# Self-attention of a decoder layer: the first copy of a tile's turned probabilities moved ahead in ScalarE's order

## The chip, the cores and the metric

The kernel runs on one core of a Trainium2 chip. The time is that of one execution on the device in microseconds (us), the median of several runs. Beside it there is one profiled execution with a trace of every instruction. The engines are PE (TensorE, matmuls), DVE (VectorE), ACT (ScalarE), POOL (GpSimd) and SP (SyncE, which only issues DMAs here). Each runs its own list of instructions in order; they wait for one another by semaphores.

## The reference

One decoder layer on 2048 tokens of width 256 (32 sequences of 64), in three parts, each with a layer norm ahead and a residual behind:

```python
x = x + attn(layernorm(x))      # 16 heads of 16, quantised activations and weights
x = x + xattn(layernorm(x), ctx)  # 16 heads of 128, 64 context rows a sequence
x = x + ffn(layernorm(x))       # 8 experts of 688, the best 2 of each token
```

The change is in the first. Its projections are "bitlinear": the input is normalised, multiplied by a gain, scaled by 127 over its largest magnitude in the row, rounded to integers, and multiplied by weights that are rounded to -1, 0 and 1. Scores are taken within a sequence, softmax, values, and the output goes through a fourth bitlinear.

```python
scores = einsum('bhtd,bhsd->bhts', Q, K) / sqrt(16)
out = einsum('bhts,bhsd->bhtd', softmax(scores), V)
return bitlinear(out, wo, go)
```

## The kernel before, in words

The program has three stages in a row: the self-attention (function `attention`, to about 209 us of the trace), the cross-attention and the experts. All engines meet between stages. The self-attention also prepares operands of the later stages: ten pieces of weights and context are split into a high and a low half (`split_high` on ACT, `split_low` on POOL), and the products of value and output weights are formed and split (`value_weights`, `value_high`, `value_low`).

The tokens are 16 tiles of 128 rows (two sequences each). `attention` writes one loop over steps t = -4 to 15 for each engine, and the order of the calls in that loop is the order of the engine's work. It is a software pipeline: in step t the engines begin tile t + 4 and finish tile t. Things that are done for two tiles at once (`pair(t, lag)`) come every second step. For ACT a step is (before the change):

- `squares` (even steps): sums of squares of the attention's output, two tiles, and two small exponents of them (L327 to L331)
- `turned_probs(t, 0)`: copy of the first half of the turned probabilities out of the bank `pt` (L321), 128x512
- `value_high` (odd steps, L357), `quantise(t + 4)` (L297, three instructions, which wait for the scales of DVE's `front`), `turned_probs(t, 1)`: the copy of the second half
- `query(t + 2)` (L307), `exponent(t + 1)` (L316), `value(t + 2)` (L312), `key_scales(t + 3)` (L302)
- `quantise_out` (odd steps, L336), `split_high` (odd steps, L352 and L353, 128x1024 each)
- `second_norm` (even steps from 6 on, L340 and L341) and `h_high` (L346)

PE in a step: `turn_probs(t, 0)` (L545, 16 small matmuls, 32 rows of the trace, that turn half of the heads' probabilities into the bank `pt`), `value_weights` and `project_out` (odd steps), `scores(t + 1)` (L560), `turn_probs(t, 1)`, which must wait until ACT has copied the first half out of the same bank, `project(t + 2)` (L572), `values(t + 2)` (L580), `key_scales(t + 3)` (L586), and `outputs(t)` (L596, probabilities times values), which needs both halves copied. `turn_probs(t + 1, 0)` comes behind `outputs(t)` and needs the exponents of tile t + 1.

DVE in a step: `front(t + 4)` (L426 to L432, the input with gain, and its scales), `residual` and `value_low` (odd), `shifted(t + 1)` (L449, L452), `keys(t + 2)` (L444), `out_scale` (odd, L466 to L472), `second_stats` (even), `integers(t + 4)` (L438), `outputs(t)` (L457, L461), `out_integers` (odd, L477, which waits for `quantise_out`), `hidden` (even from 6 on, L500, which waits for `second_norm`). All of it is in that order whatever comes ready first.

The copy and its waits are these:

```python
def turned_probs(i, part):
    act.wait_ge(p_done, 2 * i + part + 1)
    need(act, o_done, i)
    nc.scalar.copy(pT[:, 8 * part:8 * part + 8, :]...,
                   pt[:, :]).then_inc(pT_done, 1)
```

`p_done` counts PE's turned halves, `o_done` its `outputs`.

Of the kernel before, what the change touches and what calls it, by code (L numbers as in the profile page):

```python
# [92 lines left out]
def need(engine, semaphore, count):  # L93

    if count > 0:
        engine.wait_ge(semaphore, count)


def attention(nc, sem, dram, x_sb, cst, ao, hT, wq, wk, wvo, cT, ck, carry):
# [5 lines left out]
    with ctx:  # L105
# [67 lines left out]
        def tile(i):  # L173
            return 0 <= i < NT

        def pair(t, lag):

            j, rest = divmod(t - lag, 2)
            return j if rest == 0 and 0 <= j < NPAIRS else None
# [8 lines left out]
        with nc.Block() as block:  # L188
# [81 lines left out]
            def _(act):  # L270
# [23 lines left out]
                def quantise(i):  # L294
                    act.wait_ge(sc_done, 2 * i + 2)
                    for j in range(QKV):
                        nc.scalar.activation(u[:, j, :], u[:, j, :], ACT.Identity, scale=qsc[:, i, j:j + 1], bias=magic).then_inc(yq_done, 1)  # L297

                def key_scales(i):
                    act.wait_ge(t_done, i + 1)  # L300
                    need(act, kf_done, i - 1)
                    nc.scalar.copy(dk[i % 2][:, :], g0[:, 0:P]).then_inc(zT_done, 1)  # L302

                def query(i):
                    act.wait_ge(q_done, i + 1)
                    need(act, s_done, i - 1)
                    nc.scalar.copy(q_f[i % 2][:, :, :].rearrange("p m n -> p (m n)"), qb[:, :]).then_inc(qf_done, 1)  # L307

                def value(i):
                    act.wait_ge(v_done, i + 1)  # L310
                    need(act, o_done, i - 2)
                    nc.scalar.activation(vb[i % 3][:, :, 0:D1], g2[:, 0:C].rearrange("p (h d) -> p h d", d=D1), ACT.Identity, scale=deq[:, i, 2:3]).then_inc(vb_done, 1)  # L312

                def exponent(i):
                    act.wait_ge(sub_done, i + 1)
                    nc.scalar.activation(sp[i % 2][:, :, :], sp[i % 2][:, :, :], ACT.Exp, scale=deq[:, i, 0:1]).then_inc(exp_done, 1)  # L316
# [4 lines that stand above are left out]
                    nc.scalar.copy(pT[:, 8 * part:8 * part + 8, :].rearrange("p h n -> p (h n)"), pt[:, :]).then_inc(pT_done, 1)  # L321

                def squares(j):
                    act.wait_ge(ao_done, 2 * j + 2)
                    for a in range(2):
                        need(act, sq_done, 2 * j + a)
                        nc.scalar.activation(junk[:, :], ao2[j % 2][:, a, :], ACT.Square, accum_out=ssq[:, j, a:a + 1]).then_inc(sq_done, 1)  # L327
                    act.wait_ge(sq_done, 2 * j + 2)
                    links.link(nc.scalar.activation(ln_o[:, j, :], ssq[:, j, :], ACT.Ln, scale=1.0 / C, bias=cst[:, CONSTS + 1:CONSTS + 2]))
                    nc.scalar.activation(rms_o[:, j, :], ln_o[:, j, :], ACT.Exp, scale=0.5).then_inc(rms_done, 1)  # L330
                    nc.scalar.activation(rrms_o[:, j, :], ln_o[:, j, :], ACT.Exp, scale=-0.5).then_inc(rms_done, 1)  # L331

                def quantise_out(j):
                    act.wait_ge(so_done, 2 * j + 2)
                    for a in range(2):
                        nc.scalar.activation(ug[:, a, :], ug[:, a, :], ACT.Identity, scale=qsc_o[:, j, a:a + 1], bias=magic).then_inc(yo_done, 1)  # L336

                def second_norm(j):
                    act.wait_ge(st_done, 2 * j + 2)
                    links.link(nc.scalar.activation(ln_h[:, j, :], mv_o[:, j, :, 1], ACT.Ln, bias=cst[:, CONSTS:CONSTS + 1]))  # L340
                    nc.scalar.activation(rstd_h[:, j, :], ln_h[:, j, :], ACT.Exp, scale=-0.5, bias=cst[:, CONSTS + 6:CONSTS + 7]).then_inc(rs_done, 1)  # L341

                def h_high(j):
                    act.wait_ge(h_done, 2 * j + 2)
                    need(act, hT_in, 32 * j)
                    nc.scalar.copy(hp[:, :, 0, :], h[:, :, :]).then_inc(hh_done, 1)  # L346

                def split_high(n):
                    act.wait_ge(raw_in[n % 2], (n // 2 + 1) * 16)
                    src, high, low, up, parts = splits[n]  # L350
                    part = raw[n % 2][:, :].rearrange("p (a n) -> p a n", a=parts) if parts > 1 else raw[n % 2][:, :]
                    nc.scalar.mul(high, part, up).then_inc(high_done, 1)  # L352
                    nc.scalar.mul(part, part, up).then_inc(up_done, 1)  # L353

                def value_high(n):
                    act.wait_ge(vo_done, n + 1)
                    nc.scalar.mul(wvo[:, 0, 2 * n:2 * n + 2, :], g1[:, :].rearrange("p (h o) -> p h o", h=2), W_UP).then_inc(vo_high, 1)  # L357

                for t in steps:
                    if pair(t, 2) is not None:  # L360
                        squares(pair(t, 2))
                    if tile(t):
                        turned_probs(t, 0)
                    if pair(t, 1) is not None:
                        value_high(pair(t, 1))
                    if tile(t + 4):
                        quantise(t + 4)
                    if tile(t):
                        turned_probs(t, 1)
                    if tile(t + 2):  # L370
                        query(t + 2)
                    if tile(t + 1):
                        exponent(t + 1)
                    if tile(t + 2):
                        value(t + 2)
                    if tile(t + 3):
                        key_scales(t + 3)
                    if pair(t, 3) is not None:
                        quantise_out(pair(t, 3))
                    if t % 2 and 0 <= (t + 3) // 2 < NSPLIT:  # L380
                        split_high((t + 3) // 2)
                    if pair(t, 6) is not None:
                        second_norm(pair(t, 6))
                        h_high(pair(t, 6))
# [1573 lines left out]
```

## Time and profile before

| | |
|---|---|
| three runs | 847.98, 848.79, 852.25 us, median 848.79 |
| the profiled execution | 852.5 us, its span in the trace 850.4 us |
| busy in the span | PE 722.7, DVE 568.7, ACT 453.9, POOL 382.5 us |
| mean granted TensorE clock | 0.935 of 2.4 GHz |
| the self-attention | from the start to about 209 us |

Times of the trace count from the span's start. In a row of a timeline the first number is when the instruction (or a group of the same line, "x32") started, the second how long it took, and in brackets stands how long the engine had been idle before it and what ended that.

### The profile page before, as it was taken

Reading aid. Unit: us, or ns where it says so; the run is one execution under the profiler, and the core shown is the slowest. Engines: PE = TensorE matmul, PEld = TensorE weight load, DVE = VectorE, ACT = ScalarE, POOL = GpSimd, SP = SyncE. Lnnn points to the kernel's source line nnn. Section 1 sums busy time; section 2 is a strip of 40 time slices with the busy share of each in tenths; the row PEclk is TensorE's granted clock in tenths of the full one; section 3 lists DMA queues with packets and bytes.
Section 4 is the critical chain, followed back from the end, with each engine's and each line's share of the span. In section 5 each row is a group of like instructions: output and inputs, shape, how many; then the busy total and the mean of one; then the engine's idle time right before and its main releaser. Section 6 shows DMA issues by size and latency. Waiting matters only on the chain. (4 is left out here: it accounts for less than half of the span.)

```text
span 850.4 us, 26921 instructions
## 1 busy us (share of the span) xinstructions
PE 722.7 (85%) x10796; PEld 522.1 (61%) x10796; DVE 568.7 (67%) x1052; ACT 453.9 (53%) x875; POOL 382.5 (45%) x462
## 2 busy tenths in 40 slices
PE   0499888887887999999999996988199999998993
PEld 0388777775443566656556664766167777776772
DVE  5778788863886989999898997967853333332330
ACT  0567777764785666667675763544023333333331
POOL 0112222322585555555555555620056666665753
PEclk9879999995998999999999998999599999999997
DMA  9312222321664757576757573619949988889882
GB/s 323 112 50 56 59 52 64 66 58 20 168 194 156 186 127 180 135 187 160 191 128 173 163 167 112 223 31 406 369 89 158 149 147 143 142 128 137 145 140 40
DMA packets 192471, 121.91 MB, mean 143 GB/s; under 512 B 140800, under 2 KB 172800, under 8 KB 192224
## 3 DMA queue, kind: packets, MB, share of 16 engines
q1 hardware_dynamic: 178928, 103.54, 50.3%
q0 software_dynamic: 7488, 9.32, 7.1%
q10 hardware_dynamic: 5936, 7.34, 2.5%
q8 instruction: 90, 1.47, 0.7%
q14 instruction: 29, 0.24, 0.1%
HBM read 61.04 MB, written 27.00 MB: 104 GB/s over the span
## 5 line engine op out<-in xcount | busy, mean ns | idle before, releaser
L1754 DVE SCALAR_TENSOR_TENSOR f_slot_work<-psu,f_slot_work 128x688 f32<-128x688 f32 x39 | 34.1, 875 | 109.8 <-PE psu L1825 109.8
L1350 PE MATMUL xbank_a<-arena,x_o 128*128 128x256 f16 x768 | 96.6, 277 | 5.7 <-DVE x_o L1155 2.9
L1572 POOL DMA_INDIRECT out_dram<-f_y,f_to x39 | 62.2, 1595 | 71.8 <-DMA out_dram<-f_y,f_to 55.4
L1350 PEld LDWEIGHTS xbank_a<-arena,x_o 128*128 128x128 f16 x768 | 73.4, 99 | 28.7 <-DVE x_o L1155 10.3
L1254 PE MATMUL xbank_qk<-arena 128*128 128x512 f16 x336 | 84.8, 390 | 4.6 <-PEq L188 4.3
L1841 PE MATMUL fbank<-arena,f_slot_work 128*128 x663 | 79.2, 274 | 3.3 <-DMA f_slot_work<-hid_hl 3.3
L1825 PE MATMUL psg<-wgu,f_slot_work 128*128 x468 | 74.7, 309 | 2.5 <-DMA f_slot_work<-rows_in 2.0
L1825 PE MATMUL psu<-wgu,f_slot_work 128*128 x468 | 74.6, 309 | 0.0
L1841 PEld LDWEIGHTS fbank<-arena,f_slot_work 128*128 128x128 f16 x663 | 64.7, 98 | 14.6 <-issue 4.3
L1622 ACT CAST hid_hl<-f_slot_work 128x688 f16<-128x688 f32 x39 | 29.8, 765 | 77.4 <-DVE f_slot_work L1754 75.4
L915 POOL TENSOR_TENSOR arena<-arena,cst 128x512 f32<-128x512 f32 x25 | 26.0, 1039 | 92.2 <-DVE cT L1190 92.2
L961 ACT ACTIVATE sqq<-xbank_qk 128x512 f32<-128x512 f32 x56 | 33.3, 595 | 56.3 <-PE xbank_qk L1254 56.3
L1615 ACT ACTIVATE f_slot_work<-psg 128x688 f32<-128x688 f32 x39 | 29.0, 743 | 64.4 <-PE psg L1825 63.1
L545 PE MATMUL bank_pt<-cst,sp 64*64 64x64 f32 x1024 | 42.8, 242 | 21.6 <-ACT pT L321 19.4
L1825 PEld LDWEIGHTS psg<-wgu,f_slot_work 128*128 128x128 f16 x468 | 45.4, 98 | 23.4 <-issue 3.8
L1825 PEld LDWEIGHTS psu<-wgu,f_slot_work 128*128 128x128 f16 x468 | 45.8, 98 | 22.5
L1757 DVE TENSOR_TENSOR hid_hl<-f_slot_work,hid_hl 128x688 f16<-128x688 f32 x39 | 34.2, 877 | 32.4 <-ACT hid_hl L1622 32.4
L545 PEld LDWEIGHTS bank_pt<-cst,sp 64*64 64x64 f32 x1024 | 38.4, 154 | 23.9 <-issue 20.5
L1254 PEld LDWEIGHTS xbank_qk<-arena 128*128 128x128 f16 x336 | 28.7, 99 | 36.8 <-issue 8.0
L1145 DVE TENSOR_TENSOR q_hl<-xbank_qk,q_hl 128x512 f16<-128x512 f32 x56 | 38.4, 686 | 16.9 <-ACT q_hl L962 16.9
L1262 PE MATMUL xbank_qk<-cT,wk 128*128 128x512 f16 x168 | 47.1, 391 | 0.0
L904 POOL TENSOR_TENSOR x_pf<-x_sc,x_rden 128x512 f32<-128x512 f32 x32 | 33.4, 1042 | 29.8 <-DVE x_rden L1178 29.8
(285 smaller groups left out, 1717.5 us busy)
## 6 DMA issues: line engine op xcount, KB each, us to landing
arena<-in_wx SPq DMA_DIRECT2D x51, 256.0 KB, 3.0
wgu<-w_hl SPq DMA_DIRECT2D x2, 5504.0 KB, 26.5
ao<-key_norms SPq DMA_DIRECT2D x64, 128.0 KB, 3.3
w_hl<-cT SPq DMA_DIRECT2D x26, 256.0 KB, 2.1
w_hl<-x_pair SPq DMA_DIRECT2D x25, 256.0 KB, 2.2
ao<-in_wx SPq DMA_DIRECT2D x10, 256.0 KB, 3.2
w_hl<-ao SPq DMA_DIRECT2D x10, 256.0 KB, 2.1
x_sb<-in_x SPq DMA_DIRECT2D x4, 512.0 KB, 9.6
```

The lines of the kernel that those rows point to most:

```text
L545: last = nc.tensor.matmul(pt[rows, n * S:(n + 1) * S], sp[i % 2][rows, 8 * part + n, :], cst[rows, IDENT + S * b:IDENT + S * b + S], start ...
L904: nc.gpsimd.tensor_tensor(pf[:, :, :], sc[n % 2][:, :, :], rden[n % 2][:, :].unsqueeze(2).to_broadcast([P, 2 * GT, S]), ALU.mult).then_inc ...
L961: nc.scalar.activation(sqq[h % 2][:, :], query_bank(h), ACT.Square, scale=1.0 / (H_UP * W_UP)).then_inc(sq_done, 1)
L1145: nc.vector.tensor_tensor(q_hl[:, 1, slot(h), :], query_bank(h), q_hl[:, 0, slot(h), :], ALU.subtract).then_inc(lq_done, 1)
L1254: last = nc.tensor.matmul(query_bank(h), wq[:, a, k, f:f + D2], hT[:, g, b * NCH + k, :], start=(j == 0), stop=(j == len(terms) - 1))
L1262: last = nc.tensor.matmul(key_bank(h), wk[:, a, f:f + D2], cT[:, g, b, :], start=(j == 0), stop=(j == 2))
L1350: last = nc.tensor.matmul(acc[t // 2][:, (t % 2) * C:(t % 2 + 1) * C], o_hl[h % 2][:, a, at:at + P], wvo[:, b, e, :], start=(e == 0 and j ...
L1572: nc.gpsimd.indirect_dma_start(out=dram["out_rows"], out_offset=bass.IndirectOffsetOnAxis(ap=to[n % 2][:, 0:1], axis=0), in_=y[n % 2][:, : ...
L1754: nc.vector.scalar_tensor_tensor(out=h3, in0=psu[:, :].rearrange("p (c n) -> p c n", c=2)[:, :, 0:FH], scalar=HID_UP / (H_UP * W_UP), in1= ...
L1757: nc.vector.tensor_tensor(hid_hl[n % 2][:, 1, 0:FF], hid[n % 2][:, :], hid_hl[n % 2][:, 0, 0:FF], ALU.subtract).then_inc(s["hh_low"], 1)
L1825: last = nc.tensor.matmul(bank[:, c * 512:c * 512 + FH], xT[n % 2][:, b * NCH + k, :], wgu[:, bass.ds(e, 1), at:at + FH].rearrange("p a n ...
L1841: last = nc.tensor.matmul(ps[n % 2][:, 0:C], hidT[n % 3][:, a, f, :], wd[:, bass.ds(e, 1), at:at + C].rearrange("p a n -> p (a n)"), start ...
```

## The change

Both calls at the head of ACT's step are moved. The copy of the first half is now made for tile t + 1 at the end of step t, behind `key_scales`, and so a step earlier in the list: ahead of `quantise_out`, `split_high`, `second_norm` and `h_high` of step t. The squares stay in their step, but go from its head to behind that copy.

```diff
                 for t in steps:
-                    if pair(t, 2) is not None:
-                        squares(pair(t, 2))
-                    if tile(t):
-                        turned_probs(t, 0)
                     if pair(t, 1) is not None:
                         value_high(pair(t, 1))
...
                     if tile(t + 3):
                         key_scales(t + 3)
+                    if tile(t + 1):
+                        turned_probs(t + 1, 0)
+                    if pair(t, 2) is not None:
+                        squares(pair(t, 2))
                     if pair(t, 3) is not None:
                         quantise_out(pair(t, 3))
```

In the lists that follow `u` is the tile being quantised, `pT` and `bank_pt` the turned probabilities and their bank, `a_raw` a piece to split, `ao` and `k_hl` space that holds the attention's output, the quantised output and the hidden rows, `per_pair` small numbers of a pair. First ACT from the end of step 9 into step 10, before:

```order
L302 COPY dk<-bank_g 128x128
L336 ACTIVATE k_hl<-k_hl,cst,per_pair 128x256 x2
L352 ACTIVATE cT<-a_raw 128x2x512
L353 ACTIVATE a_raw<-a_raw 128x1024
L327 ACTIVATE k_hl,per_pair<-ao_0 128x256 x2
L329 ACTIVATE per_pair<-per_pair,cst 128x2
L330 ACTIVATE per_pair<-per_pair 128x2
L331 ACTIVATE per_pair<-per_pair 128x2
L321 COPY pT<-bank_pt 128x512
L297 ACTIVATE u<-u,cst,qsc 128x256 x3
L321 COPY pT<-bank_pt 128x512
```

The same place in the changed kernel:

```order
L302 COPY dk<-bank_g 128x128
L321 COPY pT<-bank_pt 128x512
L336 ACTIVATE k_hl<-k_hl,cst,per_pair 128x256 x2
L352 ACTIVATE cT<-a_raw 128x2x512
L353 ACTIVATE a_raw<-a_raw 128x1024
L297 ACTIVATE u<-u,cst,qsc 128x256 x3
L321 COPY pT<-bank_pt 128x512
```

The copy of tile 10's first half (the first L321) has passed quantising and weight piece, and the squares (L327 to L331) have left this place.

ACT at the end of step 10, before:

```order
L302 COPY dk<-bank_g 128x128
L340 ACTIVATE per_pair<-k_hl,cst 128x2
L341 ACTIVATE per_pair<-per_pair,cst 128x2
L346 CAST k_hl<-k_hl 128x2x256
L321 COPY pT<-bank_pt 128x512
L357 ACTIVATE arena<-bank_g 128x512
```

and in the changed kernel:

```order
L302 COPY dk<-bank_g 128x128
L321 COPY pT<-bank_pt 128x512
L327 ACTIVATE k_hl,per_pair<-ao_0 128x256 x2
L329 ACTIVATE per_pair<-per_pair,cst 128x2
L330 ACTIVATE per_pair<-per_pair 128x2
L331 ACTIVATE per_pair<-per_pair 128x2
L340 ACTIVATE per_pair<-k_hl,cst 128x2
L341 ACTIVATE per_pair<-per_pair,cst 128x2
L346 CAST k_hl<-k_hl 128x2x256
L357 ACTIVATE arena<-bank_g 128x512
```

Here tile 11's copy and the squares of step 10 stand ahead of the second norm (L340, L341), which stood directly behind L302. The lists of PE, DVE, POOL and SP are the same in both kernels.

## Rows read from the trace of the kernel before

**Rows 1.** Waits of PE inside the self-attention (us in total, times, longest).

```profile
PE bank_pt L545 <- ACT pT L321: 19.4, 7, 3.2
```

**Rows 2.** Timeline of PE, steps 10 to 12 (start, us, engine, line).

```profile
143.76 1.15 PE L545 MATMUL bank_pt<-cst,sp 64*64 64x64 f32 x32 [0.30 <-ACT sp L316]
...
149.74 1.97 PE L545 MATMUL bank_pt<-cst,sp 64*64 64x64 f32 x32 [3.19 <-ACT pT L321]
...
153.75 2.04 PE L596 MATMUL bank_g<-vb,pT 64*64 64x17 f32 x64
155.63 1.13 PE L545 MATMUL bank_pt<-cst,sp 64*64 64x64 f32 x32
...
158.19 1.72 PE L560 MATMUL bank_s<-k_f,q_f 32*64 32x64 f32 x64
159.84 1.15 PE L545 MATMUL bank_pt<-cst,sp 64*64 64x64 f32 x32
...
162.36 2.04 PE L596 MATMUL bank_g<-vb,pT 64*64 64x17 f32 x64
164.70 1.15 PE L545 MATMUL bank_pt<-cst,sp 64*64 64x64 f32 x32 [0.30 <-ACT sp L316]
```

**Rows 3.** Timeline of ACT, steps 9 to 10.

```profile
144.54 1.09 ACT L336 ACTIVATE k_hl<-k_hl,cst,per_pair 128x256 f32<-128x256 f32 x2 [0.32 <-DVE per_pair L472]
...
147.44 0.40 ACT L327 ACTIVATE k_hl<-ao 128x256 f32<-128x256 f32 x1
...
149.03 0.57 ACT L321 COPY pT<-bank_pt 128x512 f32<-128x512 f32 x1
149.50 1.58 ACT L297 ACTIVATE u<-u,cst,qsc 128x256 f32<-128x256 f32 x3
...
155.08 0.30 ACT L340 ACTIVATE per_pair<-k_hl,cst 128x2 f32<-128x2 f32 x1 [0.20 <-DVE k_hl L492]
155.41 0.30 ACT L341 ACTIVATE per_pair<-per_pair,cst 128x2 f32<-128x2 f32 x1
```

**Rows 4.** Timeline of DVE, steps 9 and 10.

```profile
145.67 0.43 DVE L477 TENSOR_SCALAR k_hl<-k_hl 128x512 bf16<-128x512 f32 x1
...
148.41 0.19 DVE L432 SCALAR_TENSOR_TENSOR deq<-amax,norm,wm 128x3 f32<-128x3 f32 x1
...
156.47 0.73 DVE L500 TENSOR_SCALAR k_hl<-x_sb,k_hl,per_pair 128x256 f32<-128x256 f32 x2
```

**Rows 5.** Timelines of PE and DVE, the first pairs.

```profile
63.82 1.13 PE L545 MATMUL bank_pt<-cst,sp 64*64 64x64 f32 x32
...
71.84 2.04 PE L596 MATMUL bank_g<-vb,pT 64*64 64x17 f32 x64
...
91.26 2.19 PE L596 MATMUL bank_g<-vb,pT 64*64 64x17 f32 x64
...
101.91 1.13 PE L545 MATMUL bank_pt<-cst,sp 64*64 64x64 f32 x32
...
83.28 0.43 DVE L477 TENSOR_SCALAR k_hl<-k_hl 128x512 bf16<-128x512 f32 x1
...
103.64 0.43 DVE L477 TENSOR_SCALAR k_hl<-k_hl 128x512 bf16<-128x512 f32 x1
...
114.49 0.73 DVE L500 TENSOR_SCALAR k_hl<-x_sb,k_hl,per_pair 128x256 f32<-128x256 f32 x2
```

**Rows 6.** Timelines of DVE, PE and POOL, the last pairs and the stage's end.

```profile
177.19 0.73 DVE L500 TENSOR_SCALAR k_hl<-x_sb,k_hl,per_pair 128x256 f32<-128x256 f32 x2
...
192.88 3.60 PE L596 MATMUL bank_g<-vb,pT 64*64 64x17 f32 x64 [0.67 <-ACT pT L321]
...
207.05 2.12 POOL L257 TENSOR_TENSOR ck<-a_raw,ck 128x1024 f16<-128x1024 f32 x1 [7.28 <-ACT a_raw L353]
```

**Rows 7.** A row of PE's timeline; busy by stretch (PE, PEld, DVE, ACT, POOL, granted clock, DMA).

```profile
67.86 1.97 PE L545 MATMUL bank_pt<-cst,sp 64*64 64x64 f32 x32 [1.26 <-ACT pT L321]
...
149.74:153.20 3.46, 3.46 (x48) 3.34 (x49) 1.22 (x1) 2.41 (x5) 2.37 (x2) 0.52 0.19 43
```

## The prediction, made before the changed kernel ran

> **What bounds the kernel now.** I first asked whom TensorE waits for inside the self-attention. The table of waits [rows 1] names the first copy of turned probabilities, line 321: 19.4 us in 7 waits. That is all the change can take away directly. Then I read one pair of tiles, t = 10 and 11, on the timelines of three engines. I write tp0(t), tp1(t) for TensorE's two turns of a tile's probabilities (L545), TP0, TP1 for ScalarE's copies of them (L321), outputs(t) for L596, hidden(t) for VectorE's L500 in step t.
>
> On PE [rows 2] tp0(10) starts at 143.76, and tp1(10) only at 149.74, after 3.19 us idle and at half clock (1.97 us, where 159.84 shows 1.15). Outputs(10) starts at 153.75, tp0(11) at 155.63. From tp1(11) at 159.84 to outputs(11) at 162.36 PE needs 2.52 us when nothing stops it. On ACT [rows 3] the copy for which PE waits starts at 149.03, because output quantising and a weight piece (144.54 to 147.44, 2.90 us) and the squares (147.44 to 149.03, 1.59 us) lie ahead of it. The second norm is at 155.08, 0.63 us to the end of its last row. On DVE [rows 4] L477 (the integers of the output) starts at 145.67, 1.13 us after ACT's quantising, the scales of tile 14 are done at 148.60, and hidden(10) starts at 156.47. The pair comes round in some 21.0 us: tp0(12) is at 164.70 [rows 2].
>
> **The change, part by part.** No instruction is added or removed. On ACT 16 copies of 0.58 us stand elsewhere, and 7 groups of squares. PE, DVE, POOL and SP issue the same rows in the same order, so no DMA is passed by another. Two waits of others change hands.
>
> *TP0 goes ahead of quantising and weight piece (all pairs).* Gain: PE no longer waits for it; the stall of 3.19 us goes. Price: ACT now waits for PE at that place, and what is queued behind the copy comes later. Behind it is the quantising of the output (L336), for which DVE waits at L477, and behind L477 stands L426 to L432, the scales of the next tile. Worked for t = 10: tp0 ends near 144.9, the copy takes ACT until 145.43 (0.05 to start, 0.48 to the next, as 149.03 to 149.50), quantising starts 0.89 later than before, so L477 at 146.56 and the scales at 149.49. ACT is free at 145.43 + 2.90 = 148.33 and must wait for them: the quantising of tile 14 (L297) starts at 149.50, exactly as before. Its 1.50 us and the copy TP1 (0.58) give outputs(10) at 151.65, 2.1 us earlier than 153.75.
>
> *Squares go behind the next TP0, and so does the second norm.* This is the new wait. Outputs(10) at 151.65, tp0(11) 1.88 later at 153.53, its end and the copy 1.15 + 0.05 + 0.48 later: 155.2. Then squares 1.59, second norm 0.63, and 0.08 to DVE: hidden(10) starts at 157.5, against 156.47 before. DVE, which has its own outputs(10) done some 0.7 us after PE's (151.65 + 2.04 + 0.7 = 154.4), stands still for 3 us, and behind hidden is the next tile's L426. So the 3.19 us stall is paid back with 1.0 us on top: a pair that has a second norm takes 22.0 us. In the present trace that norm hid in ACT's wait for tp0(11); that cover is gone.
>
> *The sum by pairs, with TensorE at full clock.* The second norm is only there for t = 6, 8, 10, 12, 14.
> - t = 2: from tp0(2) at 63.82 [rows 5], 1.13 + 0.05 + 0.48, weight piece 1.9 (2.90 less the 1.0 of L336), tile quantising 1.50, copy 0.63: outputs(2) at 69.5 instead of 71.84. PE then has no gap, so tp0(4) is 2.2 earlier, at 79.7.
> - t = 4: L477 at 79.7 + 1.66 + 1.1 = 82.45 (83.28 before), scales 2.93 later, outputs(4) at 87.5 instead of 91.26; tp0(6) 3.85 earlier, at 98.05 (101.91 before).
> - t = 6: the same way L477 100.8 (103.64), outputs(6) 105.9, hidden(6) 5.86 later (1.88 + 1.68 + 1.59 + 0.63 + 0.08) at 111.8 instead of 114.49: 2.7 ahead.
> - t = 8 and 10: 1.0 lost each. Ahead 0.7.
> - t = 12 has no tile to quantise: TP1(12) is at 169.3, PE is ready at about 170.4 itself, hidden(12) at 176.3 instead of 177.19 [rows 6]: 0.9 gained. Ahead 1.6.
> - t = 14: hidden(12) to tp0(14) is the 8.23 us from hidden(10) to tp0(12) less 2.5 for the missing scales plus 0.4 for ACT's copies: 6.15. Then 1.68, 2.90 and 0.63: outputs(14) 11.4 after hidden(12), against 15.7 (192.88 - 177.19). It takes 2.04 instead of 3.60 if the clock is up: 5.85 gained.
> - Tail: the stage ends with POOL's last low piece, which starts 10.6 us after outputs(14) ended (207.05 against 192.88 + 3.60). Squares, second norm, hidden and two copies now follow tp0(15) in a row: about 0.5 more.
> Sum: 2.7 - 2.0 + 0.9 + 5.85 - 0.5 = 6.95 us faster. What follows the stage starts after its last engine and moves as a block; I cost it at nothing.
>
> *The clock.* A stall that goes should also take away the slow stretch behind it, but the walk leaves new gaps on PE. From the start of tp0(10) PE needs 1.08, the scores' 1.65 (158.19 to 159.84) and 2.52, together 5.25 us, to be ready for outputs(10), that is at 149.0, and gets its copy at 151.6: a gap of 2.6 us, and it lies straight ahead of outputs(10) and tp0(11), which are on the path. A second one of about 2 us is before outputs(11). [Rows 7]: behind 1.26 us idle tp1(2) ran at 1.97 us a group, so a gap shorter than these sufficed for the fall to 1.2 GHz; 0.30 us before tp0(10) did not. A fall lasts about 3.4 us (granted 0.52 from 149.74 to 153.20), which costs at most 3.46 x 0.48 = 1.7 us. Bounds for the even gap: 0 (it falls into work with slack) and 1.7; I take 1.3, since 3.2 us of path work stand right behind it. For the odd gap 0 and 1.2; I take 0.5, since outputs(11) has 0.9 us of slack before tp0(12). Count: t = 4 at 1.7 (PE is the bound right after), t = 6, 8, 10 at 1.3, odd gaps at t = 7, 9, 11 at 0.5, and 2.35 at t = 14 and the tail (outputs(14) at 3.60 as now, and 0.8 on tp0(15)): 9.45 us. It is as large as everything else together.
>
> The Trainium skill ("TensorE: Matmul & The Clock Gate", section "Why this matters for your kernels") ties the fall to idle gaps longer than any that I work out here. By that rule the 9.45 us would be nothing and the change would come out 7 us faster. The 1.26 us row speaks against it, so it is only a rival.
>
> **Sum:** 6.95 - 9.45 = -2.5, that is 2.5 us slower. The profiled execution took 852.5 us (span 850.4 and 2.1 around it), 3.7 above the median of 848.79; a difference worked out in the one I add to the other: 851.3 us.
>
> **The rivals.**
> *The clock stays up:* no cost behind the gaps, 848.8 - 6.95 = 841.8 us. For it: the new gaps are shorter than 3.19 us and lie spread. Against it: the 1.26 us row. 0.14.
> *Slower, the clock falls behind both gaps of every pair at its full price:* 4 x 1.7, 3 x 1.2, 2.35 and 1.0 at t = 12 make 13.75, and the time 855.6 us. For it: the even gap is followed by nothing but path work. Against it: slow stretches eat the next gap. It decides from a clock cost of 11.2 us on (6.95 + 4.25), that is when the even gap costs 1.7 and the odd one about 1. 0.26.
> *Nothing takes the place of the stall:* the whole 19.4 us go, 829.4 us. Against it: DVE's order puts hidden ahead of the next tile, and ACT's order the norm behind the squares. 0.04.
>
> **How the numbers follow.** The forecast, a change of little size, has 0.56; its own range is 848 to 854.5. Half a per cent, 4.2 us, is about what a measurement of this kernel can tell from no change, so "same" is 844.6 to 853.0. Faster: 0.14 + 0.04 = 0.18. Slower: 0.26 and 0.07 of the forecast's upper end, 0.33. Same: 0.49. The range reaches to most of both clock rivals: 843.5 to 856.5; what is left out is the fastest part of the first, the top of the second and the last.
>
> **What would show it.** Right: the waits of tp1 for L321 are gone; DVE waits 3 us before hidden (L500) on L341 in five steps; ACT waits for tp0 before every first copy; L477 waits for L336; outputs(even) waits for TP1; pairs t = 8 and 10 come round in 22.0 us at full clock and 23 to 24 with slow stretches, and those before t = 6 in less than now. Wrong: if hidden doesn't wait for the norm; if outputs(even) starts without a gap; if the pairs from t = 8 on take 21 us or less; if the stages behind the self-attention change their length by over a microsecond.

## The result, and the profile after

| | before | changed |
|---|---|---|
| median | 852.20 us (20 runs) | 856.29 us (20 runs) |
| ratio | | 1.0053, 95% interval 1.0031 to 1.0075 |
| profiled execution, span | 850.4 us | 850.3 us |
| mean granted TensorE clock | 0.935 | 0.923 |
| TensorE busy | 722.7 us | 731.3 us |

The changed kernel is slower by half a per cent: 4.5 us on the 848.79 that the prediction started from (2.6 to 6.4), so 853.3 us. One of the 20 executions of the kernel before took 1354 us, and the ratio leaves it out. The 853.3 us lie in the range, just above what I called "same" (844.6 to 853.0), and the likeliest case, no change that a measurement can tell, was not what came: the interval leaves no change out. The sum itself said 2.5 us slower, so its direction was right and its size was not.

One trace of each doesn't show the difference in the span, because the first two tiles happened to take 3.9 us less in the changed kernel's trace (tp0(2) starts at 59.92 against 63.82 [rows 5]), where the order is all but the same; in a second trace of the changed kernel (e8 below) tp0(2) starts at 63.86. Counted from tp0(2) to the end of POOL's last low piece the self-attention took 145.35 us before and 151.80 after.

The waits inside the self-attention, in the changed kernel (us in total, times, longest):

```profile
PE bank_g L596 <- ACT pT L321: 8.3, 8, 2.6
...
DVE k_hl L500 <- ACT per_pair L341: 16.4, 5, 3.8
...
DVE k_hl L477 <- ACT k_hl L336: 8.8, 6, 1.8
...
ACT pT L321 <- PE bank_pt L545: 29.6, 18, 4.3
```

The 19.4 us in which PE waited for the first copy [rows 1] are gone. In their place PE waits 8.3 us for the second copies ahead of outputs, DVE waits 16.4 us at hidden for the second norm, which it never did, and 8.8 us at L477 for the output quantising. ACT itself waits 29.6 us for PE's turned halves.

PE's timeline in the same pair, t = 10 and 11, and the next (start, us, engine, line, idle before):

```profile
143.73 1.97 PE L545 MATMUL bank_pt<-cst,sp 64*64 64x64 f32 x32 [0.57 <-ACT sp L316]
...
148.36 1.97 PE L545 MATMUL bank_pt<-cst,sp 64*64 64x64 f32 x32
...
152.85 2.04 PE L596 MATMUL bank_g<-vb,pT 64*64 64x17 f32 x64
154.74 1.13 PE L545 MATMUL bank_pt<-cst,sp 64*64 64x64 f32 x32
...
162.82 0.38 PE L580 MATMUL bank_g<-k_hl,zT 128*128 128x256 bf16 x2 [1.73 <-DVE x_sb L483]
...
164.03 2.04 PE L596 MATMUL bank_g<-vb,pT 64*64 64x17 f32 x64 [0.55 <-ACT pT L321]
166.90 1.97 PE L545 MATMUL bank_pt<-cst,sp 64*64 64x64 f32 x32 [0.83 <-ACT sp L316]
...
176.10 2.25 PE L596 MATMUL bank_g<-vb,pT 64*64 64x17 f32 x64
178.20 1.12 PE L545 MATMUL bank_pt<-cst,sp 64*64 64x64 f32 x32
```

ACT's in the same pair:

```profile
145.75 0.59 ACT L321 COPY pT<-bank_pt 128x512 f32<-128x512 f32 x1 [1.55 <-PE bank_pt L545]
146.23 1.09 ACT L336 ACTIVATE k_hl<-k_hl,cst,per_pair 128x256 f32<-128x256 f32 x2
...
150.32 1.58 ACT L297 ACTIVATE u<-u,cst,qsc 128x256 f32<-128x256 f32 x3 [1.10 <-DVE deq L432]
151.81 0.56 ACT L321 COPY pT<-bank_pt 128x512 f32<-128x512 f32 x1
...
155.91 0.59 ACT L321 COPY pT<-bank_pt 128x512 f32<-128x512 f32 x1 [1.49 <-PE bank_pt L545]
...
158.32 0.30 ACT L341 ACTIVATE per_pair<-per_pair,cst 128x2 f32<-128x2 f32 x1
```

DVE's, with hidden(8), hidden(10) and hidden(12):

```profile
135.49 0.74 DVE L500 TENSOR_SCALAR k_hl<-x_sb,k_hl,per_pair 128x256 f32<-128x256 f32 x2 [2.81 <-ACT per_pair L341]
...
147.36 0.43 DVE L477 TENSOR_SCALAR k_hl<-k_hl 128x512 bf16<-128x512 f32 x1 [1.78 <-ACT k_hl L336]
...
158.65 0.73 DVE L500 TENSOR_SCALAR k_hl<-x_sb,k_hl,per_pair 128x256 f32<-128x256 f32 x2 [2.99 <-ACT per_pair L341]
...
182.11 0.73 DVE L500 TENSOR_SCALAR k_hl<-x_sb,k_hl,per_pair 128x256 f32<-128x256 f32 x2 [2.99 <-ACT per_pair L341]
```

Compare with [rows 2 to 4]. tp0(10) starts at 143.73, by chance almost where it did before (143.76), so the numbers can be read side by side. TP0(10) is now at 145.75, L336 at 146.23 instead of 144.54, and L477 follows it at 147.36 instead of 145.67. The quantising of the next tile starts at 150.32 (149.50), TP1(10) at 151.81 and outputs(10) at 152.85, still 0.9 earlier than 153.75. But TP0(11), squares and second norm now stand in a row, 155.91 to 158.62, and hidden(10) starts at 158.65 instead of 156.47.

The granted clock in two stretches of the changed kernel and, third, in one of the kernel before (us, PE, PEld, DVE, ACT, POOL busy, then clock and DMA):

```profile
142.48:152.72 10.24, 9.67 (x164) 9.14 (x160) 8.11 (x19) 7.53 (x13) 2.28 (x2) 0.50 0.35 59
166.34:176.59 10.25, 9.69 (x158) 9.06 (x158) 6.30 (x14) 7.17 (x13) 3.36 (x2) 0.50 0.39 68
...
190.66:200.88 10.22, 9.55 (x134) 8.33 (x129) 1.63 (x7) 3.79 (x7) 2.10 (x2) 0.50 0.07 15
```

Before, the slow stretch of a pair lasted 3.4 us (0.52 from 149.74 to 153.20, [rows 7]). Here two of them last 10.2 us each. The first begins at 142.5, inside outputs(9), behind gaps of 1.61 and 0.60 us; the second at 166.3, behind gaps of 1.73 and 0.55 us and inside a third of 0.83 us, in which PE waited for the exponents of tile 12. Each ends only about when outputs(even) begins: tp0, scores, tp1 and project all run at 1.2 GHz. Over the stage the falls last 6.8, 6.8, 6.8, 10.2, 10.2 and 13.7 us, and the last one 4.4 us up to the stage's end. A long stretch was there before the change, too: the third row, behind a gap of 2.86 us at tp1(14), is a part of the old trace from which the prediction took only outputs(14) at 3.60 us.

This is also why outputs(10) has no gap ahead of it: PE, at half clock from tp0(10) on, was itself ready no earlier than the copy, which ended at 152.37. The forecast gap of 2.6 us ahead of outputs(even) opened at t = 4 and 6 (2.55 us each) and not at t = 8, 10 and 12.

The stage piece by piece. "Walk" is the prediction's sum at full clock, "forecast" the same with its clock terms:

| stretch | before | walk | forecast | after |
|---|---|---|---|---|
| tp0(2) to tp0(4) | 18.09 | 15.9 | 15.9 | 15.74 |
| tp0(4) to tp0(6) | 20.00 | 18.35 | 20.05 | 21.49 |
| tp0(6) to hidden(6) | 12.58 | 13.75 | 15.05 | 16.03 |
| hidden(6) to hidden(8) | 21.03 | 22.0 | 23.8 | 22.31 |
| hidden(8) to hidden(10) | 20.95 | 22.0 | 23.8 | 23.16 |
| hidden(10) to hidden(12) | 20.72 | 19.8 | 20.3 | 23.46 |
| hidden(12) to the end of outputs(14) | 19.29 | 13.45 | 15.0 | 15.82 |
| from there to POOL's end | 12.69 | 13.2 | 14.0 | 13.79 |
| sum | 145.35 | 138.45 | 147.9 | 151.80 |

### The profile page after: what moved, and what is told of

Read it like the earlier page. It is cut to its first block and busy times, and to the rows that moved or that the text cites. A ratio compares the mean times of both kernels' runs of the same rounds, so it can differ in the third digit from the quotient of the medians.

```text
span 850.3 us, 26921 instructions
## 1 busy us (share of the span) xinstructions
PE 731.3 (86%) x10796; PEld 528.4 (62%) x10796; DVE 569.5 (67%) x1052; ACT 453.1 (53%) x875; POOL 379.2 (45%) x462
## 5 line engine op out<-in xcount | busy, mean ns | idle before, releaser
L545 PE MATMUL bank_pt<-cst,sp 64*64 64x64 f32 x1024 | 44.9, 250 | 5.0 <-ACT sp L316 5.0
L1155 DVE SCALAR_TENSOR_TENSOR x_o<-xbank_o,x_o 128x512 f16<-128x512 f32 x55 | 37.8, 687 | 11.1 <-ACT x_o L972 11.1
```

The costliest lines, as they stand in the source:

```text
L545: last = nc.tensor.matmul(pt[rows, n * S:(n + 1) * S], sp[i % 2][rows, 8 * part + n, :], cst[rows, IDENT + S * b:IDENT + S * b + S], start ...
L1155: nc.vector.scalar_tensor_tensor(out=o_hl[h % 2][:, 1, :].rearrange("p (b n) -> p b n", b=2), in0=ob_of(h)[:, :, 0:RW], scalar=1.0 / P_UP, ...
```

## The experiments

Two things moved together: the copy, and the squares, which took the second norm with them by standing ahead of it. And beside the waits there is the clock. The theory was: the new waits of DVE (for the norm at hidden, for the quantising at L477) take the place of the stall, and slow stretches behind the new gaps take the rest. The first rival was that the clock alone cost, the second that every delay of the norm costs what it saves.

All edits are to ACT's loop unless another place is named. Ratios are to the kernel before, run beside each on the same chip; the pairs are from hidden(6) to (8), (10), (12) and (14) in the trace, and the stage from tp0(2) to POOL's end, with the granted clock in it:

| kernel | median us | ratio (95%) | pairs, us | stage, us (clock) |
|---|---|---|---|---|
| before | | 1 | 21.03, 20.95, 20.72, 19.97 | 145.35 (0.88) |
| changed | 856.29 | 1.0053 (1.0031 to 1.0075) | 22.31, 23.16, 23.46, 20.40 | 151.80 (0.81) |
| e1 norm first | 841.58 | 0.9885 (0.9855 to 0.9915) | 20.04, 21.33, 17.04, 15.79 | 135.01 (0.88) |
| e2 copy alone | 859.37 | 1.0057 (1.0024 to 1.0090) | 21.49, 22.36, 19.23, 19.31 | 152.62 (0.83) |
| e3 squares alone | 840.52 | 0.9882 (0.9824 to 0.9940) | 19.91, 19.91, 19.91, 17.00 | 133.73 (0.87) |
| e5 norm, then squares | 836.02 | 0.9775 (0.9725 to 0.9825) | 19.46, 18.13, 19.46, 16.93 | 129.80 (0.92) |
| e6 copy behind quantising | 833.87 | 0.9817 (0.9763 to 0.9870) | 18.18, 18.50, 16.28, 14.83 | 120.29 (0.98) |
| e7 copy ahead of quantising | 844.28 | 0.9870 (0.9815 to 0.9924) | 20.01, 21.34, 17.03, 16.99 | 135.95 (0.88) |
| e4 all gaps filled | 854.49 | 1.0015 (0.9977 to 1.0053) | 23.13, 22.50, 21.88, 18.54 | 147.61 (0.95) |
| e10 even gap filled | 864.21 | 1.0105 (1.0043 to 1.0166) | 25.63, 25.07, 26.21, 22.40 | 158.04 (0.83) |
| e11 both gaps, fewer | 860.63 | 1.0079 (1.0043 to 1.0115) | 24.52, 24.96, 24.27, 21.17 | 154.39 (0.86) |
| e12 e5 and a filled gap | 833.45 | 0.9769 (0.9727 to 0.9811) | 18.19, 20.77, 17.77, 16.36 | 126.80 (0.95) |

**e1, the norm ahead of the copy.**

```diff
 # on the changed kernel
                         key_scales(t + 3)
+                    if pair(t, 6) is not None:
+                        second_norm(pair(t, 6))
                     if tile(t + 1):
                         turned_probs(t + 1, 0)
...
                     if pair(t, 6) is not None:
-                        second_norm(pair(t, 6))
                         h_high(pair(t, 6))
```

> The changed kernel with the second norm (L340, L341) ahead of the next tile's first copy instead of behind the squares; the cast of the hidden rows stays at the step's end. Theory (what takes the place of the removed stall is DVE's wait for the second norm, 16.4 us in 5 waits): these waits go, a pair with a norm comes round about 3 us sooner at full clock, and the whole is 10 to 15 us faster than the changed kernel, ratio to the kernel before 0.985 to 0.995. Rival (only TensorE's slow stretches behind the new gaps cost): the gap before outputs(even) stays 2.5 us, the stretches stay, and the time is within 3 us of the changed kernel's.

It came to 841.58 us, ratio 0.9885, some 1.7% under the changed kernel. A wait of DVE, two rows of DVE's timeline (L478 is L477 here, L501 is L500) and outputs(10) on PE:

```profile
DVE k_hl L478 <- ACT k_hl L336: 8.2, 6, 1.5
...
141.62 0.43 DVE L478 TENSOR_SCALAR k_hl<-k_hl 128x512 bf16<-128x512 f32 x1 [1.50 <-ACT k_hl L336]
...
150.97 0.73 DVE L501 TENSOR_SCALAR k_hl<-x_sb,k_hl,per_pair 128x256 f32<-128x256 f32 x2
...
146.69 3.60 PE L597 MATMUL bank_g<-vb,pT 64*64 64x17 f32 x64 [2.55 <-ACT pT L321]
```

The waits at hidden are gone (no idle time before 150.97), while L477's are nearly as they were (8.2 for 8.8 us). Outputs(10) now has a gap of 2.55 us ahead of it, as outputs(4) and outputs(6) have in the changed kernel too, and runs at half clock. About 14 us went (1.7% by the two ratios), so the time is the theory's and not the rival's. But the clock did not stay as it was. From tp0(2) to the stage's end, in the kernel before, the changed one, e1 and e4 (below):

```profile
63.82:209.17 145.35, 119.79 (x2920) 110.23 (x2916) 105.12 (x219) 99.68 (x207) 37.95 (x30) 0.88 0.25 54
...
59.92:211.72 151.80, 130.22 (x2920) 118.73 (x2917) 106.74 (x219) 98.71 (x207) 38.16 (x30) 0.81 0.23 52
...
60.23:195.24 135.01, 118.24 (x2920) 107.78 (x2916) 106.56 (x219) 98.39 (x207) 38.00 (x30) 0.88 0.29 58
...
62.96:210.57 147.61, 137.62 (x3148) 123.55 (x3145) 107.00 (x219) 98.39 (x207) 38.16 (x30) 0.95 0.25 53
```

Twice the length, times what the clock lacks to 1, is the time at 1.2 GHz: about 35, 58, 32 and 15 us. So e1 took away the norm's waits and some 25 us of slow clock together, and alone it can't part the two. e4 parts them roughly: it keeps the waits at hidden (15.2 us) and takes away more slow time than e1, and its stage is 4.2 us shorter than the changed kernel's, where e1's is 16.8 us shorter. The larger part of e1's gain is therefore that of the waits; how much exactly isn't shown, since e4 pays for its fillers.

**e2, the copy alone** (squares back at the head of ACT's step).

```diff
 # on the changed kernel
                 for t in steps:
+                    if pair(t, 2) is not None:
+                        squares(pair(t, 2))
                     if pair(t, 1) is not None:
...
                         turned_probs(t + 1, 0)
-                    if pair(t, 2) is not None:
-                        squares(pair(t, 2))
```

> The changed kernel with the squares back at the head of ACT's step; only the copy is moved. Theory: the norm then waits for the copy alone, hidden comes 1.6 us sooner and the tile's quantising starts up to 0.5 us later, so about 1.1 us a pair, 5 to 8 us faster than the changed kernel, ratio to before 0.995 to 1.000. Rival (the copy ahead of output quantising is what costs, by way of L477): no change against the changed kernel, ratio 1.005.

1.0057, the rival's number: no gain over the changed kernel. Waits of PE and DVE:

```profile
PE bank_g L596 <- ACT pT L321: 16.6, 7, 2.9
...
DVE k_hl L500 <- ACT per_pair L341: 10.2, 5, 2.2
DVE k_hl L477 <- ACT k_hl L336: 7.6, 6, 1.9
```

Hidden waits 2.2 us where it waited 2.8 to 3.8, so 0.6 to 1.6 us less a wait (10.2 in five), but PE's waits for the second copies doubled to 16.6 us. That this is because the squares stand ahead of the next tile's quantising is my reading of the order. The pairs from hidden(6) on are shorter, while what lies before is longer: hidden(6) starts 60.8 us after tp0(2), against 53.3 in the changed kernel, at a granted clock of 0.76 against 0.87, with one slow stretch of 17 us in it. So both places tried for the squares with the copy moved cost about as much: ahead of the norm and ahead of the quantising.

**e3, the squares alone** (the copy at its old place).

```diff
 # on the kernel before
                 for t in steps:
-                    if pair(t, 2) is not None:
-                        squares(pair(t, 2))
                     if tile(t):
                         turned_probs(t, 0)
...
                         key_scales(t + 3)
+                    if pair(t, 2) is not None:
+                        squares(pair(t, 2))
                     if pair(t, 3) is not None:
```

> The kernel before with only the squares moved behind the key scales; the copy stays at the head of the next step. Theory: PE's stall for the first copy shrinks from 3.2 to 1.6 us, DVE's hidden waits about 1 us for the norm, and a pair is some 1 us shorter: 4 to 7 us faster than before, ratio 0.992 to 0.996. Rival (every delay of the norm costs what it saves): ratio 0.999 to 1.003, with 1.6 us of waits before hidden.

0.9882, better than expected. The waits, and tp1(10) in the same pair:

```profile
PE bank_pt L545 <- ACT pT L321: 5.2, 5, 1.4
...
DVE k_hl L500 <- ACT per_pair L341: 2.2, 3, 1.2
...
140.09 1.97 PE L545 MATMUL bank_pt<-cst,sp 64*64 64x64 f32 x32 [0.51 <-ACT pT L321]
```

PE's stall for the first copy fell from 19.4 to 5.2 us, tp1 waits 0.51 us where it waited 3.19, and hidden waits for the norm only 2.2 us in three steps. Three of the four pairs take 19.91 us. The clock has hardly a part in it: 0.87 in the stage against 0.88 before, while the stage is 11.6 us shorter. So the half of the change that moved the squares gains 1.2% by itself, and moving the copy as well turns that into a loss of 0.5%.

**e5, the norm first, then the squares, the copy at its old place.**

```diff
 # on e3
                         key_scales(t + 3)
+                    if pair(t, 6) is not None:
+                        second_norm(pair(t, 6))
                     if pair(t, 2) is not None:
                         squares(pair(t, 2))
...
                     if pair(t, 6) is not None:
-                        second_norm(pair(t, 6))
                         h_high(pair(t, 6))
```

> The kernel before with the squares moved to the step's end, behind the second norm (which keeps its place) and ahead of the cast of the hidden rows; the copies stay. Theory: both waits go, PE's for squares (3.2 us down to at most 1.4) and DVE's for the norm (2.2 us in all in the run with the squares ahead of it): 0 to 3 us faster than that run, ratio to before 0.984 to 0.990. Rival (the norm's place is worth nothing once the copy stays): same as that run, 0.988, with DVE idle for PE instead.

836.02 us, 0.9775: both kernels are beaten, the changed one by 2.8%. The ratio is below the range that I gave. It puts e5 9 us below e3, where the stages in the two traces differ by 3.9 us, and the two intervals touch. DVE no longer waits for the norm. What is left of PE's wait (L546 is L545 here), and tp1(even) of one pair:

```profile
PE bank_pt L546 <- ACT pT L321: 8.5, 6, 1.6
...
138.51 1.15 PE L546 MATMUL bank_pt<-cst,sp 64*64 64x64 f32 x32 [1.58 <-ACT pT L321]
```

**e7, the copy ahead of the output quantising, and e6, behind it,** both on e5. Only the copies for even tiles move here, which pass the quantising and the weight piece; those for odd tiles stay at the head of the step. Nothing delays the norm.

```diff
 # on e5; e7 as here, e6 with the two calls in the other order
-                    if tile(t):
+                    if tile(t) and t % 2:
                         turned_probs(t, 0)
...
+                    if t % 2 and tile(t + 1):
+                        turned_probs(t + 1, 0)
                     if pair(t, 3) is not None:
                         quantise_out(pair(t, 3))
```

> As before that, but the copy ahead of output quantising, as in the changed kernel. It shows the price of the copy's move alone, without any delay of the norm. Theory: DVE waits 1 us or more at L477 in six steps, the next tile's scales come that much later: 4 to 9 us slower than with the copies at their old place, ratio 0.991 to 0.999. Rival (only the norm behind the squares cost in the change): within 2 us of the run with the copies at their old place.

> As the run with norm, then squares, and in odd steps the next tile's first copy between output quantising and weight piece. Theory: L477 is not delayed and PE's last waits for L321 go (5.2 us in five waits), but the next tile's quantising still waits for DVE's scales, so 0 to 3 us faster than that run, ratio 0.981 to 0.989. Rival: the gap only moves to outputs(even), as in the changed kernel, with slow stretches behind it: slower than that run by 1 to 4 us.

e7 took 844.28 us, 0.9870, against 0.9775 for e5. Its waits (L599 and L480 are L596 and L477 here):

```profile
PE bank_g L599 <- ACT pT L321: 12.5, 7, 2.5
...
DVE k_hl L480 <- ACT k_hl L336: 9.1, 6, 1.7
```

PE's 8.5 us at tp1 are gone, DVE has 9.1 us at L477 instead and PE 12.5 us at outputs, against 1.6 in e5. That is the copy's price without the norm, about 1% by the ratios, whose intervals just touch; the stage is 6.2 us longer, and its lower clock (0.88 against 0.92) is a part of that. With the quantising first (e6) L477 doesn't wait (0.5 us, as before the change), and the time, 833.87 us and 0.9817, can't be told from e5. The trace says more than that: e6's four pairs are 6.2 us shorter together than e5's, at a granted clock of 0.98 in the stage against 0.92, while its tp0(2) starts 6.2 us later (68.85 against 62.69), behind first tiles that ran at 1.2 GHz until 67.1. Whether such first tiles belong to e6's order or fell that way in this one execution wasn't tried, so whether passing the weight piece alone gains anything stays open.

**e4, e10, e11, the clock.** On the changed kernel, matmuls whose results nobody reads were put on PE, into free columns of a bank that PE owns at that moment.

```diff
 # in PE's part
+                def busy(bank, count):
+                    for _ in range(count):
+                        nc.tensor.matmul(bank[:, 272:512], w_int[:, 0, 0:P], w_int[:, 1, 0:240], start=True, stop=True)
...
                 def outputs(t, i):
+                    need(pe, ao_done, i)
+                    need(pe, vo_low, passed(t, 1))
+                    if i > 3:
+                        busy(g1, 20 if i % 2 == 0 else 12)   # e10: 20, 0; e11: 20, 5
```

In e4 six more stand before tp0(even). The two waits ahead of the fillers are ones that outputs has anyway, asked for earlier.

> The changed kernel with matmuls of no use (128x240, into free columns of a bank that PE owns at that time) in the gaps that it opened: 20 before outputs(even), 12 before outputs(odd), 6 before tp0(even), from tile 4 on. Theory (slow stretches behind the new gaps cost about 10 us of the stage): granted clock 1.00 there, the pairs t = 8 and 10 come round in 22.0 us, and the whole is 7 to 11 us faster than the changed kernel, ratio to before 0.993 to 0.998. Rival (the waits of DVE alone cost, the slow stretches hide in slack): within 2 us of the changed kernel, ratio 1.005.

> The changed kernel with 20 matmuls of no use (128x240) in the gap before outputs(even) alone, from tile 4 on, none elsewhere. Theory (slow stretches behind that gap cost about 1.5 us a pair or more, and the additions elsewhere in the earlier run with busy gaps cost 0.5 us a pair themselves): 5 to 9 us faster than the changed kernel, ratio to before 0.995 to 1.001. Rival: the slow stretches move behind the odd gap, 1.003 to 1.006.

> The changed kernel with 20 matmuls of no use before outputs(even) and 5 before outputs(odd), none before tp0, so that both new gaps are filled without delaying what follows. Theory (slow stretches behind the odd gap cost as much as those behind the even one): pairs t = 8 and 10 in 22.0 to 22.6 us, ratio to before 0.996 to 1.002, better than with the even gap alone (1.0105) by 5 us or more. Rival (useless matmuls only shift the slow stretches): pairs over 23 us, ratio above 1.003.

From hidden(8) to hidden(10), first the changed kernel (in each row the stretch and its length, then PE, PEld, DVE, ACT, POOL busy, clock, DMA):

```profile
135.49:158.65 23.16, 20.38 (x450) 18.73 (x442) 17.68 (x37) 15.46 (x33) 5.77 (x5) 0.78 0.31 56
```

With all gaps filled (e4):

```profile
138.44:160.94 22.50, 21.16 (x462) 18.45 (x456) 17.59 (x37) 15.45 (x33) 5.76 (x5) 0.93 0.23 52
```

The clock is up at 0.93 from 0.78, the pair takes 22.50 us, and the walk had said 22.0 at full clock; the rest I put down to the fillers (outputs(9) and tp0(10) each start some 0.7 us late behind them, partly hidden). From tp0(2) the stage took 147.6 us instead of 151.8, and the whole was measured at 1.0015 instead of 1.0053. That misses my forecast (0.993 to 0.998, clock 1.00), and by time alone e4 decides nothing: its interval holds the changed kernel's 1.0053 as well. It is the trace that says that the slow stretches cost about 4 us at the least. The waits of DVE are still there (15.2 us at hidden, 10.9 at L477). How much more the clock costs is hidden by the fillers that stand on PE's path.

The other two missed by more. e10, rows of PE around the odd gap, and the pair:

```profile
142.34 0.38 PE L587 MATMUL bank_g<-k_hl,zT 128*128 128x256 bf16 x2 [1.72 <-DVE x_sb L483]
...
143.85 3.32 PE L607 MATMUL bank_g<-vb,pT 64*64 64x17 f32 x64 [0.91 <-issue]
...
202.26 3.86 PE L541 MATMUL bank_g<-k_hl 128*128 128x240 bf16 x20
...
138.17:163.24 25.07, 22.43 (x464) 20.83 (x456) 17.68 (x38) 15.45 (x33) 5.76 (x5) 0.80 0.38 55
```

e11, the pair:

```profile
137.27:162.23 24.96, 23.10 (x469) 21.18 (x461) 17.69 (x37) 15.46 (x33) 5.77 (x5) 0.79 0.29 55
```

Filling the even gap alone, or the odd one with too little, left the gap of 1.7 us before values of the odd step. The clock fell behind it, at 144.2 (e10) and 143.6 (e11), and PE came late to the 20 matmuls of no use before outputs(10). These took 2.2 us at full clock and up to 3.9 us in a slow stretch (the row at 202.26), and stood on the path themselves. The pairs shown are 1.9 and 1.8 us longer than the changed kernel's 23.16. Over the whole program the two ratios stand 4.4 and 2.2 us above its 1.0053, but their intervals overlap with its own, so it is the pairs that tell. What they show is that the odd gap, which I had priced at 0.5 us, is the one with the long slow stretch behind it.

**e12, e5 with 14 such matmuls ahead of tp1(even).**

```diff
 # in PE's turn_probs, on e5
                     pe.wait_ge(exp_done, i + 1)
+                    if part and i % 2 == 0 and i > 1:
+                        need(pe, ao_done, i)
+                        busy(g1, 14)
```

> The run with norm, then squares, and the copies at their old place, with 14 matmuls of no use ahead of tp1(even), where PE waits up to 1.6 us for the copy. Theory: the clock stays at its upper level there and pairs come round in 18 to 19 us, 1 to 5 us faster than without them, ratio 0.972 to 0.982. Rival: the gap is too short to matter, or the matmuls delay tp1 where no wait was: 0 to 4 us slower.

0.9769 against 0.9775: no difference that can be told. The pairs didn't all come in at 18 to 19 us; one took 20.77, with a slow stretch of 6.8 us in it. In e5 the gap of 1.58 us did not always bring the clock down (its tp1(10) above ran in 1.15 us).

**e8 and e9, both kernels once more.**

> The changed kernel once more, for a second trace. Theory: the waits of DVE at hidden (3 us in each of five steps) and at L477 (1 us or more in six) are the same to 0.3 us, since they come from the order; the slow stretches lie elsewhere, and the pairs between hidden(6) and hidden(12) differ by up to 2 us each from the first trace. Ratio 1.003 to 1.008. Rival (the placing of slow stretches is fixed by the program too): each pair within 0.3 us of the first trace.

> The kernel before once more, one look. Theory: the pairs from t = 8 on come round in 20.7 to 21.3 us again, since slow stretches follow the same single stall of 3.2 us a pair; the first two tiles may take up to 4 us less or more, as the clock lies there.

The changed kernel gave 857.39 us, ratio 1.0049 (1.0021 to 1.0077). Hidden(10) in its second trace:

```profile
162.58 0.73 DVE L500 TENSOR_SCALAR k_hl<-x_sb,k_hl,per_pair 128x256 f32<-128x256 f32 x2 [2.99 <-ACT per_pair L341]
```

Its pairs are 22.29, 23.18, 23.47, 20.39 us, each within 0.02 of the first trace; DVE's waits are the same too (16.4 and 8.8 us). The kernel before repeats as well (21.03, 20.99, 20.75, 19.94; a single execution, 847.7 us). My expectation that slow stretches wander between executions was wrong in these traces: from tp0(4) on they fall into the same place of the program in both traces of each kernel (in the changed one the first begins 24.5 us behind tp0(2) in either). Only the first tiles differ (tp0(2) at 61.02 and 63.86 in these traces).

## Why the prediction was wrong, point by point

- *Which waits go and which come:* right for three of four. The stall of tp1 went, hidden waits for L341 in five steps by 2.8 to 3.8 us (3 forecast), and L477 for L336. The gap ahead of outputs(even), on which the clock's price was built, came at t = 4 and 6 and not at t = 8, 10 and 12. That outputs(even) starts without a gap stood among my own signs of being wrong.
- *The walk at full clock:* right as far as it can be checked. The stretch that had no slow clock in it, tp0(2) to tp0(4), took 15.74 us against 15.9. In e4 tp0(6) to hidden(6) ran at full clock and took 13.67 us against 13.75, and hidden(10) to hidden(12), at 0.99, 21.88 against 19.8 with 2.1 us of fillers straight ahead of outputs(12).
- *"A fall lasts about 3.4 us, which costs at most 1.7 us":* this step failed. It took the length of the slow stretch from the pairs of the kernel before, where one gap is followed by nothing but work, and passed over the 10.2 us from 190.66 on in the same trace. In the changed kernel several gaps follow each other, and the stretches are 6.8 to 13.7 us long (10.24 and 10.25 at 0.50 in the pairs shown). What the walk leaves over, and what I put down to the clock, is 13.35 us (151.80 - 138.45), not 9.45. Of that e4 shows 4.2 us directly, after paying for its fillers; the rest is the difference to a sum that its pieces at full clock bear out.
- *Where it costs:* the even gap was priced at 1.3 and the odd at 0.5 in every pair. At t = 8 and 10 that was too much (0.3 and 1.2 measured over the walk, against 1.8): the slow work from tp0 to project mostly filled the time in which PE would have waited for TP1. At t = 12 I had put 0.5, and it was 3.7 us: with no tile to quantise PE itself is the bound from tp0(12) to outputs(12), 9.20 us instead of the 5.2 that e4 needs up to its fillers, so each lost microsecond is on the path. Even the slower rival had only 1.0 more there. At t = 4 it was 3.1 instead of 1.7: a slow stretch of 6.8 us began inside outputs(4), and from there to tp0(6) PE shows no idle row.
- *The verdict:* from these 3.9 us (13.35 less 9.45). With 13.35 for the clock the sum is 6.4 us slower, 855.2 us (853.3 measured), and the likeliest case would have been "slower".
- *The Trainium skill's rule* ("TensorE: Matmul & The Clock Gate", section "Why this matters for your kernels"), by which gaps of this length would leave the clock alone, would have given 7 us faster. The trace contradicts it here: no idle row of PE in steps 2 to 12 of the changed kernel is longer than 2.55 us, and the clock was at 0.50 for 10.2 us twice.
- *"What follows the stage moves as a block":* the span behind POOL's last piece was 641.2 and 640.6 us before, 638.6 and 640.3 after, so to within 2 us.

What stays open: from tp0(2) on the stage is 6.4 us longer in the first pair of traces and 7.8 in the second, the measured difference is 4.5 (2.6 to 6.4). The first tiles and the rest of the span vary by 2 to 4 us between traces; whether the change gives back some 2 us there wasn't settled. How the loss divides between DVE's waits and the clock is known only roughly, from e1 and e4. Nor was a kernel tried in which the changed order runs wholly at full clock without fillers on the path.

## What to carry to other kernels

Before moving an instruction ahead of others, list what it will itself wait for: in an engine that works in order everything behind it inherits that wait. Here a copy that waits for PE was put ahead of two things for which DVE waits, and the cure for PE's stall was to take away what stood ahead of the copy (the squares, which nobody needs soon), not to move the copy. When an edit takes away a wait, read the clock of the stage as well before the whole gain is put down to the wait: e1 lost both. Price the clock by the pattern of gaps that will be there, not by the slow stretch that the old pattern shows, and look first where TensorE alone is the bound.

## What the runs showed of the hardware

- Slow stretches of TensorE can be far longer than the gaps ahead of them: with gaps of 1.73, 0.55 and 0.83 us, and matmuls between them, it ran 10.2 us at 1.2 GHz, where one gap of 3.19 us was followed by 3.4 us. It stayed slow although it had work: of the 10.24 us from 142.48 on it was busy for 9.67.
- They repeat. In two traces of the same kernel, for both kernels, the pairs agree to 0.04 us, although the first tiles of the changed kernel ran 4 us apart.
- Behind a gap of 1.26 us (tp1(2), kernel before) the group ran at half clock, and behind one of 1.58 us (tp1(10), e5) at full clock. Behind 3.19 us the stretch was 3.4 us long and behind 2.86 us, in the same trace, 10.2. The length of the last gap alone doesn't decide it.
- Matmuls that fill a gap cost more when the clock is low (20 of 128x240 took 2.2 us at full clock, 3.9 in a slow stretch) and then delay the work they were to protect.
